# Cross residual, statistics and norm chain moved to earlier places, and the cross keys' middle and low parts moved from VectorE to ScalarE and GpSimd

## The reference, cut to what matters

```python
x = layernorm(x + self_attention(x))         # q, k normed and rotated, causal
x = layernorm(x + cross_attention(x, ctx))   # q from x, k and v from ctx, causal and key mask
x = layernorm(x + ffn(x))                    # rmsnorm, 8 heavy chunks and a light one of 128, gelu
```

## Time and profile before

| what | us |
|---|---|
| median of 3 runs | 958.84 |
| profiled execution, its own time | 959.52 |
| its span, first to last instruction | 957.8 |
| TensorE busy | 858.8 (90%) |
| VectorE busy | 717.8 (75%) |
| ScalarE busy | 616.7 (64%) |
| GpSimd busy | 537.7 (56%) |
| one step between 3 and 14 | 53.57 |

### The profile page before, as it was taken

One profiled execution on the slowest core, in us unless ns is written; L12 is line 12 of the kernel. 1 busy time (PEld: TensorE's weight loads), 2 busy tenths in 40 slices (PEclk: granted clock), 3 DMA queues, 4 the chain that ended last, 5 costly groups with the idle time before them and its releaser, 6 DMA issues. The chain is left out here.

```text
span 957.8 us, 21423 instructions
## 1 busy us (share of the span) xinstructions
PE 858.8 (90%) x7420; PEld 656.4 (69%) x7420; DVE 717.8 (75%) x1765; ACT 616.7 (64%) x1365; POOL 537.7 (56%) x1047
## 2 busy tenths in 40 slices
PE   3368898999999999999999999999999999889887
PEld 2236565777868686777868686777868686657767
DVE  7788787878877777878878777888878778665522
ACT  1132453787867777777878777777778777676352
POOL 7554465655565765655564765656564765344142
PEclk8768898999999999999999999999999999999999
DMA  3794384636566572727466563727466653804000
GB/s 112 111 176 75 52 107 57 100 40 101 68 101 79 79 102 47 106 44 109 58 101 79 86 95 53 108 45 105 53 101 79 90 79 62 107 14 64 17 12 23
DMA packets 79659, 74.20 MB, mean 77 GB/s; under 512 B 8608, under 2 KB 78912, under 8 KB 79552
## 3 DMA queue, kind: packets, MB, share of 16 engines
q1 hardware_dynamic: 75024, 68.11, 49.5%
q10 hardware_dynamic: 4528, 4.73, 1.9%
HBM read 17.49 MB, written 4.20 MB: 23 GB/s over the span
## 5 line engine op out<-in xcount | busy, mean ns | idle before, releaser
L854 ACT ACTIVATE pr<-bank 128x384 f32<-128x384 f32 x512 | 240.6, 499 | 144.3 <-PE bank L401 143.0
L1046 DVE TENSOR_REDUCE mx<-bank 128x3 f32<-128x384 f32 x512 | 265.8, 552 | 79.2 <-PE bank L401 75.6
L1432 POOL TENSOR_SCALAR_AFFINE_SELECT pr<-pr 128x256 f32<-128x256 f32 x512 | 220.7, 445 | 136.2 <-ACT pr L854 134.6
L401 PE MATMUL bank<-w,g 128*128 128x256 f32 x576 | 171.6, 389 | 0.3 <-ACT g L874 0.3
L788 ACT ACTIVATE bank<-cmaskb 128x384 f32<-128x384 bf16 x292 | 138.2, 491 | 30.6 <-DVE mx L1046 24.5
L1456 POOL TENSOR_TENSOR xTlow<-xT,xThigh 128x512 fp32r<-128x512 f32 x16 | 20.3, 1272 | 139.9 <-ACT xThigh L788 139.9
L401 PEld LDWEIGHTS bank<-w,g 128*128 128x128 f32 x576 | 89.4, 190 | 3.9 <-ACT g L874 0.5
L401 PE MATMUL bank<-stk2k,stk2q 97*128 97x128 bf16 (+1 forms) x512 | 86.4, 252 | 5.4 <-ACT bank L788 3.8
L401 PE MATMUL bank<-cmaskb,idb 128*128 128x256 bf16 x220 | 63.5, 289 | 28.3 <-DMA stk2k<-nat1k 14.0
L874 ACT ACTIVATE g<-bank,b 128x256 f32<-128x256 f32 x144 | 65.2, 468 | 31.0 <-PE bank L401 31.0
L401 PE MATMUL bank<-stk1q,stk1k 100*128 100x256 bf16 (+1 forms) x512 | 79.5, 253 | 1.7 <-DMA stk1q<-mT 0.7
(11 more groups left out here) (171 smaller groups left out, 1828.5 us busy)
## 6 DMA issues: line engine op xcount, KB each, us to landing
stk1q<-nat1q SPq DMA_DIRECT2D x90, 128.0 KB, 4.6
stk1k<-nat1k SPq DMA_DIRECT2D x90, 128.0 KB, 4.8
stk2k<-nat2k SPq DMA_DIRECT2D x90, 128.0 KB, 4.4
stk2q<-nat2q SPq DMA_DIRECT2D x90, 128.0 KB, 5.7
xT<-in_xT SPq DMA_DIRECT2D x16, 256.0 KB, 5.2
ctxT<-in_ctxT SPq DMA_DIRECT2D x16, 256.0 KB, 5.4
x<-in_x SPq DMA_DIRECT2D x16, 256.0 KB, 5.7
out_x<-x SPq DMA_DIRECT2D x15, 256.0 KB, 2.2
```

The costliest lines, as they stand in the source:

```text
L401: return nc.tensor.matmul(out, lhsT, rhs, start=start, stop=stop, skip_group_check=check)
L854: nc.scalar.activation(pr[:, h % (2 * HG), :], ring_bank("T", a, b, h)[:, 0:3 * P], ACT.Exp, scale=HD ** -0.5)\
L1046: V.tensor_reduce(mx3[:, h, :], scored[:, 0:3 * P].rearrange("p (k t) -> p k t", k=3), AX.X, ALU.max, negate=True).then_inc(s_mx[a], 1)
L1432: G.affine_select(out=slot, in_=slot, compare_op=ALU.is_ge, fill=0.0, base=0, pattern=[[0, 2], [1, P]], channel_multiplier=-1).then_inc(s_ ...
```

## The change

1. VectorE: `residual_cross` and `statistics_cross` of f go from `maxima(2)` (heads 1 and 6) into `maxima(1)` (heads 13 and 14).
2. GpSimd: f's norm chain goes from behind `layer_norm3` to behind `x2b`; `ctxlow` goes from behind `xTlow` to right ahead of T1's masks.
3. ScalarE: `high_x` goes ahead of three bias writes and `copy_v` in S2.
4. VectorE: `scale2` follows `layer_norm(2)` directly, ahead of `max_t(2)`; TensorE's `transpose_xn` goes from head 12 of T1 to 8, ScalarE's `copy_xn` from behind exponential 13 to behind 9.
5. Cross keys: `split_rest(2, s, 1, 0)` is taken off VectorE. ScalarE casts the middle part behind exponential 11 of T2 (`MIDK_AT`), GpSimd subtracts the low part (`low_keys`) at the end of its step.
6. Last steps: `transpose_max(2)` of the last sequence at 3 for 5, and its `copy_out` behind gelu 4 for 7.

```diff
@@ TensorE, T1
-                    add(MAX2_AT, transpose_max, 2, c)
+                    add(MAX2_LAST if c == B - 1 else MAX2_AT, transpose_max, 2, c)
@@ ScalarE, S2 and T2
+                if live(i + 2) and not first(i + 1):
+                    high_x(i + 2)
                 write_bias(2, c, *BIAS2_V)
                 if live(c):
                     copy_v(2, c)
-                if live(i + 2) and not first(i + 1):
-                    high_x(i + 2)
...
                         exponential(2, c, h)
+                    if h == MIDK_AT and live(s):
+                        mid_part(2, s, 1, 0)
@@ VectorE
                     maxima(1, s, {QN_AT[0]: lambda: scaled(0), QN_AT[1]: lambda: scaled(1),
-                                  NORM2_AT: normalise_cross, SPLITQ_AT: split_cross_q, LOWQ_AT: low_cross_q})
+                                  NORM2_AT: normalise_cross, SPLITQ_AT: split_cross_q, LOWQ_AT: low_cross_q,
+                                  RESID2_AT: residual_cross, STAT2_AT: statistics_cross})
...
-                    maxima(2, c, {RESID2_AT: residual_cross, MAXT_AT: max_rows, STAT2_AT: statistics_cross})
+                    maxima(2, c, {MAXT_AT: max_rows})
...
                     layer_norm(2, f)
+                    scale2(f)
                 if live(c):
                     max_t(2, c)
                 if live(i + 1):
                     split(1, i + 1, 0, 0)
-                if live(f):
-                    scale2(f)
-                if live(i + 1):
                     split(1, i + 1, 1, 1)
...
                     divide_pair(s, 1)
-                    split_rest(2, s, 1, 0)
@@ GpSimd
+            def low_keys(b):
+                pool.wait_ge(s_mid[2], 2 * b + 1)
+                n = nat[2][1]
+                G.tensor_tensor(n[:, 2, :], rest[:, :], n[:, 1, :], ALU.subtract).then_inc(s_split[2], 1)
...
+                if live(f):
+                    inverse_deviation(2, f)
+                    inverse_norm2(f)
                 if live(i + 2):
                     pool.wait_ge(s_xhigh, i + 3)
...
-                if live(f):
-                    inverse_deviation(2, f)
-                    inverse_norm2(f)
-
                 if live(s):
+                    pool.wait_ge(s_chigh, s + 1)
+                    wait(pool, s_v[2], s)
+                    G.tensor_tensor(ctxp[1][:, :, :], ctxT[:, :, :], ctxp[0][:, :, :].bitcast(f32), ALU.subtract)\
+                        .then_inc(s_clow, 1)
                     mask_probs(1, s, {})
...
                 if l == B - 4:
                     inverse_deviation(3, l)
+                if live(s):
+                    low_keys(s)
@@ constants
-MAX2_AT, XNT_AT, XNT_LAST = 5, 12, 3
+MAX2_AT, XNT_AT, XNT_LAST = 5, 8, 3
-COPY2_LAST = 7
+COPY2_LAST, MAX2_LAST = 4, 3
-MIDQ_AT, COPY2_AT, COPY_XN_AT, COPY_V1_AT = 1, 4, 13, 15
+MIDK_AT = 11
+MIDQ_AT, COPY2_AT, COPY_XN_AT, COPY_V1_AT = 1, 4, 9, 15
-... RESID2_AT, MAXT_AT, STAT2_AT = (1, 2), 5, 6, 8, 1, 3, 6
+... RESID2_AT, MAXT_AT, STAT2_AT = (1, 2), 5, 6, 8, 13, 3, 14
```

More of the change, by code:

```diff
@@ L1238, in low_cross_q, with residual_cross, statistics_cross @@
                         low_part(2, c, 0, 1)
+                def residual_cross():
+                    if live(f):
+                        dve.wait_ge(s_x1c, f + 1)
+                        add_residual(2, f, proj_bank(2, f), x1c)
+                def statistics_cross():
+                    if live(f):
+                        statistics(2, f)
                 if live(s):
                     maxima(1, s, {QN_AT[0]: lambda: scaled(0), QN_AT[1]: lambda: scaled(1),
-                                  NORM2_AT: normalise_cross, SPLITQ_AT: split_cross_q, LOWQ_AT: low_cross_q})
+                                  NORM2_AT: normalise_cross, SPLITQ_AT: split_cross_q, LOWQ_AT: low_cross_q,
+                                  RESID2_AT: residual_cross, STAT2_AT: statistics_cross})
                     max_parts(1, s)
@@ L1249, in step @@
                     low_cross_q()
+                    residual_cross()
+                    statistics_cross()
                 if starting(i + 1):
                     rotate(dve, V, i + 1)
-                def residual_cross():
-                    if live(f):
-                        dve.wait_ge(s_x1c, f + 1)
-                        add_residual(2, f, proj_bank(2, f), x1c)
                 def max_rows():
@@ L1261, in max_rows @@
                         max_t(1, s)
-                def statistics_cross():
-                    if live(f):
-                        statistics(2, f)
                 if live(c):
-                    maxima(2, c, {RESID2_AT: residual_cross, MAXT_AT: max_rows, STAT2_AT: statistics_cross})
+                    maxima(2, c, {MAXT_AT: max_rows})
                     max_parts(2, c)
                 else:
-                    residual_cross()
                     max_rows()
-                    statistics_cross()
                 if live(f):
                     layer_norm(2, f)
+                    scale2(f)
                 if live(c):
@@ L1463, in step @@
                     pool.wait_ge(s_rows, 7)
[L1464 to L1469, removed]
                 if live(c):
@@ L1539 @@
 HIDDEN_LATE = (3, 4, 5, 6, 8, 9, 10, 12)
-COPY2_LAST = 7
+COPY2_LAST, MAX2_LAST = 4, 3
 FFN1_AT = (0, 1, 2, 3, 4, 6, 8, 9, 10)
 K2_AT, OUT1_AT, QK1_AT, V1_AT = 1, (3, 9), (3, 6), 13
-MIDQ_AT, COPY2_AT, COPY_XN_AT, COPY_V1_AT = 1, 4, 13, 15
+MIDK_AT = 11
+MIDQ_AT, COPY2_AT, COPY_XN_AT, COPY_V1_AT = 1, 4, 9, 15
 COPY1_AT, SQ_AT = (0, 3, 3), (5, 7)
-QN_AT, NORM2_AT, SPLITQ_AT, LOWQ_AT, RESID2_AT, MAXT_AT, STAT2_AT = (1, 2), 5, 6, 8, 1, 3, 6
+QN_AT, NORM2_AT, SPLITQ_AT, LOWQ_AT, RESID2_AT, MAXT_AT, STAT2_AT = (1, 2), 5, 6, 8, 13, 3, 14
 RSTD3_AT, RSTD1_AT, RSTD1_LAST = 3, 13, 10
```

## The result

The changed kernel takes 975.5 us, median of four executions (974.77 to 976.61), beside 958.72 for the kernel before: 1.0172 times as long, with a 95% interval of 1.0151 to 1.0193. The forecast was 974.9, in a range of 957 to 982. The profiled execution took 974.77, with a span of 973.0, which is 15.2 more than the 957.8 of before.

A forecast was written before the change was run, and what follows sets the result against it. TensorE's in-order stream was taken to bound the kernel, busy 51.26 of 53.57 us a step. Terms -11.5 + 5.3 + 3.5 + 7.6 + 12.2 - 1.0 = +16.1 on the median 958.84 gave 974.9 us, range 957 to 982.

The forecast's parts named there:

- norm chain off T1's start: First `values` of T1: TensorE's wait for GpSimd's masks goes, 0.77 a step and 1.51 in step 2, -11.5 us.
- residual and statistics at S1's end: Heads 14 and 15 of S1: head 1 of S2 comes 0.62 late, 0.25 a step left, +3.5 us.
- `transpose_xn` at 8: T1, steps 3 to 14: four transposes come on top of a full TensorE, 0.44 a step, +5.3 us.
- cast behind exponential 11: T2 on ScalarE, steps 1 to 14: TensorE's wait for x1 grows by 0.54 a step, +7.6 us.
- hold by `low_keys`: End of GpSimd's step, steps 1 to 13: its subtraction holds a Newton step of VectorE, 0.94 each, +12.2 us.
- `high_x`: nothing: ScalarE in S2: putting `high_x` ahead of the bias writes neither gains nor loses time.
- The wait that it was to leave ahead of the third `values`: T1 on TensorE: with the transposes taken out, a wait of about 0.6 appears there.
- VectorE is ahead enough: Rival at x1: the cast's 0.54 and GpSimd's 0.94 fall into spare time, -3.7, 955.1 us; chance 0.11.
- ScalarE hides the cast: Rival in T2: the cast costs nothing and GpSimd's part costs as a mask, -1.5, 957.3 us; chance 0.10.
- like a mask: Rival at the Newton steps: GpSimd's subtraction holds VectorE no more than a mask, 2.2 for 12.2, 964.9 us; chance 0.11.
- `max_parts` is held by the moved chain: Rival: the norm chain's two operations of 0.7 hold `max_parts(1)`, 20 us more, 994.5 us; chance 0.02.
- The end: Last steps: `copy_out` of the last sequence comes three gelus sooner, -1.0 us.

The follow-up runs named there:

- the copy and the subtraction: Copy: changed kernel with GpSimd's subtraction of the cross keys' low part replaced by a copy of the rest, 966.01 us; subtraction: the changed kernel itself, 975.5 us.
- the memset: Changed kernel with GpSimd's subtraction of the cross keys' low part replaced by a memset of the same tile: 962.52 us, 1.0028.

## Why the prediction was right

The steps in a ledger, per step of the loop. "Measured" is the difference between two of the kernels above; the sum is against the step of before, 53.57.

| step of the prediction | predicted | measured | from |
|---|---|---|---|
| norm chain off T1's start | -0.77 | -0.83 | 52.74 (`high_x` alone) - 53.57; the same wait |
| residual and statistics at S1's end | +0.25 | +0.18 | 52.92 - 52.74 |
| `transpose_xn` at 8 | +0.44 | +0.40 | 53.32 - 52.92 |
| cast behind exponential 11 | +0.54 | +0.54 | 54.74 - 54.20 |
| hold by `low_keys` | +0.94 | +0.86 | 54.74 - 53.88 |
| sum | +1.40 | +1.15 | 54.74 - 53.57 = 1.17 |

**Norm chain.** Right as to the wait that goes and its size; -0.83 is a little more than 0.77. As the cause, the text named one of two edits that each suffice. The runs with `high_x` alone and without it show that. The ledger's -0.83 is thus that of `high_x`. The chain waits for the statistics and was moved together with them: with residual, statistics and chain moved, but not `high_x`, the step is 52.94, which is 0.63 less than before. The first two lines together give 0.52 as predicted and 0.65 as measured. What was wrong is in how many steps the wait is there; that stands under the sum.

**`high_x`: nothing.** This step failed, though the sum did not, as the two edits' gains don't add up. I had looked at what the copy would delay on ScalarE and not at what it would release. What it releases is the first line of the list of waits of before, of which I read only the smaller ones: GpSimd stood 98.7 us in ten steps ahead of `xTlow`, waiting for `xThigh`, and everything up to the masks stood behind it without a pause. An idle time can cost nothing and its end can still set the start of a run that is late.

**S1's end.** The size was right, and it has two parts of opposite sign: the residual there gains 0.35, the statistics lose 0.53. The prediction took them as one block of 1.5, which is 0.62 late and gives 0.34 back. By these runs its 0.34 is the residual's part, and what is late is the statistics'. In the changed kernel head 1 waits 0.72 for its bias write, and head 4's wait is gone, as the text said.

**`transpose_xn`.** Right. The wait that it was to leave ahead of the third `values` is smaller than I said: the scores ahead of them wait 0.25 for an exponential, and the `values` 0.13 more for a mask; 0.6 was expected. Of the 0.25 by which the ledger's sum is under the forecast, 0.04 lies here, 0.06 and 0.07 in the two lines above it, and 0.08 in the hold.

**The cast, and the chain behind it.** Right to the hundredth: no slack from exponential 12 over mask 12, rstd and x1 to TensorE (0.81 for the forecast 0.8), and one place further on the cast costs nothing. The rival in which VectorE is ahead enough is out: its wait for rstd grew, from 0.68 to 1.37, as the text said against it. So is that in which ScalarE hides the cast.

**The hold.** Taken from one row at the start of the launch, 1.17 for 0.23. Measured: 1.09 for 0.23, in each steady step, with 0.98 of waiting at S1's fourth head. The rival "like a mask" is out by the copy and the subtraction. That `max_parts` is held by the moved chain didn't happen either: S2 as a whole is only 0.19 longer. But this case hardly put it to the test. The chain's two operations of 0.7 lie ahead of and behind the subtractions of `max_parts` (rstd ends at 423.47, rr begins at 424.52). The row below lies within `ss` between them (423.82, 0.25), and takes as long as an operation of its kind in before.

```profile
423.82 0.19 DVE L1060 TENSOR_TENSOR nr<-nm,mp 128x32 f32<-128x32 f32 x1
```

The Trainium skill, SBUF — State Buffer, § Who interferes with whom, has VectorE's two-input instruction and GpSimd's read of SBUF exclude each other for the whole of the one that began first. For GpSimd's operations over 256 and 512 columns the traces agree (the Newton operations are held up to the end of a mask, a copy and a subtraction, and 0.07 to 0.09 longer). For GpSimd's operations of 128x2 they don't: the earlier trace rows remains the clearest case.

**The end.** 1.07 in the trace for 1.0; its time was not told from none.

**The sum.** The profiled executions differ by 15.25 (974.77 and 959.52), 0.85 less than the forecast's 16.1. The medians differ by 16.8, since that of before lay 0.8 above its median and that of after 0.7 below. The agreement with the median to 0.6 us is thus closer than the terms deserve, and in part luck: each term is within 0.1 of its size per step, but the gain was counted in too many steps, and other errors made up for it.

The sum has the wait for masks in all steps from 2 to 15. The first `values` of T1 in steps 3 and 14 of before, and in step 15, and then the wait that is left in step 2 of the changed kernel, at its third `values`:

```profile
215.13 0.86 PE L401 MATMUL bank<-pr,va1b 128*32 128x256 f32 x16
803.71 0.86 PE L401 MATMUL bank<-pr,va1a 128*32 128x256 f32 x16
855.06 1.06 PE L401 MATMUL bank<-pr,va1b 128*32 128x256 f32 x16 [1.23 <-POOL pr L1432]
169.78 0.86 PE L401 MATMUL bank<-pr,va1a 128*32 128x256 f32 x16 [0.75 <-POOL pr L1438]
```

In step 3 GpSimd has no `layer_norm3` yet, in step 14 no `xTlow` any more, and the masks come in time without any edit. The list of waits said so: 9 times in ten steps. By these waits the term is 10 x 0.77 + 1.23 + 1.51 - 0.75 = 9.7 for the 11.5 of the sum.

By the start of S1 in consecutive steps, the changed kernel is 4.3 behind at step 4 (239.67 for 235.39), where the terms up to there give -1.51 - 0.77 + 2 x 0.25 + 0.44 + 2 x 0.54 + 2 x 0.94 = 1.6, and 15.8 ten steps on (787.02 for 771.25). It is 17.9 behind at the first scores of step 16 (906.34 for 888.48), and 15.2 at the end. The ten steps between are those of the ledger. The first ones lose 2.7 more than my terms have for them. Found there are the 0.77 of step 3 and the 0.75 of step 2; 0.83 of waiting for x1 at the start of step 1, where GpSimd's subtraction meets x1 itself (last section); and 0.96 more of waiting for the load of `stk2q` (2.48 and 1.47 for 2.40 and 0.59), of which it wasn't tried what it comes from. That is 3.3; smaller waits that went the other way weren't followed one by one. The end gives 2.7 back, of which the 1.07 above is known and the rest left open.

## What to carry to other kernels

Before an operation is given to an idle engine, look at what the neighbour does in the same stretch: 1.15 us on GpSimd that read SBUF cost the critical path 0.86, since a Newton step of 0.23 met it, while a cast on ScalarE cost 0.54 or nothing, by one place in a queue. When a wait has a long run of work behind it, look at what starts that run, even if the engine seems to have time to spare; one copy put ahead of four instructions (three bias writes and the copy of v) was worth 1% here. Split a move into its instructions before it is judged: of two that moved together, one gained 0.35 and the other lost 0.53. And before a wait of one step is multiplied, look in which steps it is there.

## What the runs showed of the hardware

A VectorE operation over 128x64 with two inputs (0.23 alone) that meets a GpSimd operation of 256 or 512 columns with an input in SBUF ends 0.07 to 0.09 us behind it, whether it is a mask (451.05 + 1.23 = 452.28; 451.94 + 0.42 = 452.36), a copy of 0.61 or a subtraction of 1.15. A memset of the same tile, 0.52 long, doesn't hold it at all (0.22). So for such an operation the price goes by whether GpSimd reads and for how long, and not by what it writes.

That isn't so for every operation of VectorE. At the start of step 1, GpSimd's new operation meets x1, which reads one tensor: its two operations in before, with nothing on GpSimd beside them, then beside the memset, then beside the subtraction of the changed kernel.

```profile
83.59 0.73 DVE L1133 TENSOR_SCALAR x<-y,mv,rstd 128x256 f32<-128x256 f32 x2
...
82.88 0.86 DVE L1135 TENSOR_SCALAR x<-y,mv,rstd 128x256 f32<-128x256 f32 x2
82.75 0.53 POOL L1429 MEMSET nat2k<- 128x512 bf16 x1
...
83.58 1.56 DVE L1135 TENSOR_SCALAR x<-y,mv,rstd 128x256 f32<-128x256 f32 x2
83.46 1.21 POOL L1429 TENSOR_TENSOR nat2k<-rest,nat2k 128x512 bf16<-128x512 f32 x1
```

They take 0.73, 0.86 and 1.56, and TensorE waits 2.12, 2.24 and 2.95 for them (one row each, as this happens once in a launch). So one input doesn't make an operation safe from GpSimd, and beside this one even the memset, which only writes, had a small price.
